# Cross attention of a fused decoder: where VectorE's maxima, an image's scaling and the weighted sums stand in the order of work

## The reference, cut to what matters

```python
q, k, v = x @ Wq + bq, y @ Wk + bk, y @ Wv + bv
weight = jax.nn.softmax(einsum('bhqd,bhkd->bhqk', q, k) / sqrt(32), axis=-1)
out = einsum('bhqk,bhkd->bhqd', weight, v)
x = _layernorm(x + out.transpose(0, 2, 1, 3).reshape(B, SQ, 256) @ Wo + bo)
```

## Time and profile before

| what | number |
| --- | --- |
| median of 3 runs | 2578.68 us (2573.37 to 2583.72) |
| the profiled execution's own time | 2584.56 us |
| its span in the profile | 2583.2 us |
| mean granted clock of TensorE | 0.906 of 2.4 GHz |
| busy: PE, DVE, ACT, POOL | 82%, 67%, 46%, 34% of the span |
| the block from its first maxima to its end | 1233.6 to about 1733 us |
| units 0 to 15 (first to last pair) | 1271.4 to 1712 us |

### The profile page before, as it was taken

How to read it: one execution, slowest core, us unless ns; L and a number is a source line. 1 busy time by engine, 2 the same in 40 slices (tenths; PEclk the granted TensorE clock), 3 DMA queues, 4 the chain that set the end, 5 groups by cost and what they waited for, 6 DMA issues and landing times. The chain is left out here.

```text
span 2583.2 us, 45827 instructions
## 1 busy us (share of the span) xinstructions
PE 2107.4 (82%) x17241; PEld 1348.7 (52%) x17241; DVE 1723.9 (67%) x3400; ACT 1191.5 (46%) x2208; POOL 872.3 (34%) x672
## 2 busy tenths in 40 slices
PE   5997579987589995887788989877787897787787
PEld 3554147874479993443344444444555554555544
DVE  4876977768966665666677777737677435777553
ACT  2132866646333332323245555445565434655552
POOL 2110024421056660012266767553221223221041
PEclk8998779999689997888899989988999998998999
DMA  4112024451351113222222322020000001000000
GB/s 145 44 49 53 1 82 132 135 171 55 128 220 50 51 46 125 76 82 89 76 75 72 94 70 70 22 76 34 1 1 1 25 1 51 1 1 1 33 9 25
DMA packets 107465, 159.63 MB, mean 62 GB/s; under 512 B 26064, under 2 KB 85236, under 8 KB 104180
## 3 DMA queue, kind: packets, MB, share of 16 engines
q1 hardware_dynamic: 102836, 144.64, 18.0%
q0 software_dynamic: 4416, 12.06, 1.6%
HBM read 109.42 MB, written 47.19 MB: 61 GB/s over the span
## 5 line engine op out<-in xcount | busy, mean ns | idle before, releaser
L2981 DVE TENSOR_REDUCE xa_max<-psum 128x1 f32<-128x1024 f32 (+1 forms) x256 | 246.4, 987 | 97.7 <-PE psum L2892 93.1
L3063 ACT ACTIVATE xa_work<-psum 128x1024 f32<-128x1024 f32 (+1 forms) x208 | 212.8, 1024 | 186.0 <-PE psum L2915 184.4
L3120 POOL TENSOR_TENSOR xa_ctx_f<-xa_ctx_f,xa_work 128x1024 f32<-128x1024 f32 x96 | 226.8, 2362 | 45.9 <-ACT xa_work L3063 37.9
L3297 PE MATMUL psum<-xa_c_parts,x_hl_f 128*128 128x512 bf16 x576 | 154.3, 417 | 63.3 <-ACT qk_raw_l L3505 24.8
L2892 PE MATMUL psum<-xa_key_rows,xa_query_rows 96*128 96x512 bf16 (+1 forms) x512 | 132.9, 352 | 36.9 <-DVE xa_max L2981 20.8
L1050 POOL TENSOR_TENSOR text_q<-text_q 128x512 bf16<-128x512 f32 x64 | 81.5, 1277 | 175.4 <-ACT text_q L1470 175.1
L2932 PE MATMUL psum<-xa_work,xa_values 128*32 128x128 f32 (+1 forms) x3328 | 140.7, 287 | 0.0
L2915 PE MATMUL psum<-xa_query_rows,xa_key_rows 98*128 98x512 bf16 (+1 forms) x416 | 130.3, 396 | 10.4 <-DVE xa_max L2981 10.4
L1802 PE MATMUL psum<-moe_rows,moe_w 128*128 128x256 bf16 x1104 | 130.4, 276 | 4.9 <-issue 4.9
L2061 ACT CAST x_ch<-moe_raw 128x512 bf16<-128x512 f32 x92 | 56.9, 618 | 158.7 <-DVE moe_raw L1976 158.2
L3297 PEld LDWEIGHTS psum<-xa_c_parts,x_hl_f 128*128 128x128 bf16 x576 | 56.3, 104 | 138.2 <-ACT qk_raw_l L3505 27.8
(11 more groups left out here) (482 smaller groups left out, 5118.7 us busy)
## 6 DMA issues: line engine op xcount, KB each, us to landing
text_q<-in_moe_w SPq DMA_DIRECT2D x64, 256.0 KB, 3.5
experts<-text_q SPq DMA_DIRECT2D x64, 256.0 KB, 2.8
moe_w<-experts SPq DMA_DIRECT2D x16, 1024.0 KB, 10.7
xa_key_rows<-cross_keys SPq DMA_DIRECT2D x48, 200.1 KB, 3.5
ctx_chunk<-in_ctxT SPq DMA_DIRECT2D x24, 300.0 KB, 3.0
cross_keys<-xa_k_hl SPq DMA_DIRECT2D x6, 800.5 KB, 3.7
moe_w<-pairs_out SPq DMA_DIRECT2D x8, 512.0 KB, 7.4
xa_ctx_f<-in_ctxT SPq DMA_DIRECT2D x4, 800.5 KB, 4.9
```

The source lines that it names most:

```text
L2981: v.tensor_reduce(t["maxes"][n % 2][:, qt * HU + a, part:part + 1], u.wide[:, 0:c1 - c0], AX.X, ALU.max).then_inc(*u.free)
L3063: act.activation(t["exps"][k % EXPS][0:rows], u.wide[0:rows].rearrange("p (m q) -> p m q", q=T), ACT.Exp, scale=1.0 / float(np.sqrt(np.flo ...
L3120: g.tensor_tensor(total, other, exps, ALU.add).then_inc(*s.added.up())
L3297: ins = pe.matmul(b.ap, x[:, i, h, w * P:(w + 1) * P], t["wqkv"][:, j, h, cols], start=(h, n) == (0, 0), stop=(h, n) == (1, 2))
```

## The change: what it does

It touches `cross_plan`, the norm's scaling and the order within a step.

```diff
+def reducing_work(step):
+    if step[0] == "maximum":
+        a, e = PARTS[step[4]]
+        return e - a + 160
+    return {"gather": 2500, "out": 700, "spread": 2000, "scale": 400, "cut": 1100, "subtract": 400}.get(step[0], 0)

 def cross_plan():
...
-    unit, lead = len(maxima) // UNITS_X, 3 * len(maxima) // UNITS_X // 2
+    lead = LATER + 2 * TPB * HU + 2
...
-            for lag, what in ((3, ("out", 0)), (4, ("out", 2)), (6, ("spread",)), (8, ("scale",)), (11, ("channels",))):
+            for lag, what in ((3, ("out", 0)), (4, ("out", 2)), (6, ("spread",)), (8, ("scale",)), (9, ("normal",)), (11, ("channels",))):
...
-    done = 0
+    total = sum(map(reducing_work, maxima)) + sum(reducing_work(step) for steps in late.values() for step in steps)
+    share, credit, done = total / (STEPS - KT), 0.0, 0
     for k in range(STEPS + BEHIND + 16):
-        if 0 <= k - BEHIND < STEPS:
-            plan.append(("product", k - BEHIND))
         plan += late.get(k, [])
+        credit += share - sum(map(reducing_work, late.get(k, [])))
         if k < STEPS:
             plan.append(("pair", k))
...
-        upto = min(len(maxima), unit * (k + 1) // KT)
-        plan += maxima[done:upto]
-        done = max(done, upto)
+        due = maxima.index(("subtract", (k + 2) // KT)) if ("subtract", (k + 2) // KT) in maxima else -1
+        while done < len(maxima) and (credit > 0 or done <= due):
+            plan.append(maxima[done])
+            credit -= reducing_work(maxima[done])
+            done += 1
+        if 0 <= k - BEHIND < STEPS:
+            plan.append(("product", k - BEHIND))
...
 cross_dve:
         elif kind == "scale":
...
             v.reciprocal(m.rstd[:, tiles], m.std[:, tiles]).then_inc(*s.v_step.up())
             v.wait_ge(*s.v_step.now())
-            for i in group(b):
-                ins = v.tensor_scalar(x[:, i, :], x[:, i, :], m.mv[:, i, 0:1], m.rstd[:, i:i + 1], ALU.subtract, ALU.mult)
-            ins.then_inc(*s.normed.up())
+            v.scalar_tensor_tensor(t["minus"][:, tiles], m.mv[:, tiles, 0], -1.0, m.rstd[:, tiles], ALU.mult, ALU.mult).then_inc(*s.centred.up())
 cross_act:
+        elif kind == "normal":
+            b, = step[1:]
+            act.wait_ge(*s.centred(b + 1))
+            for i in group(b):
+                x = m.x_tok[:, i, :]
+                ins = act.activation(x, x, ACT.Identity, scale=m.rstd[:, i:i + 1], bias=t["minus"][:, i:i + 1])
+            ins.then_inc(*s.normed.up())
```

More of the change, by code:

```diff
@@ L2751, in cross_attention @@
                  parts=ring("xa_parts", 2, [P, TPB, 2, HU], BF16), parts_t=ring("xa_parts_t", 2, [2 * HU, T], BF16),
-                 ident_b=sb("xa_ident_b", [P, P], BF16), rsum=ring("xa_rsum", 2, [P, ASKED]))
+                 ident_b=sb("xa_ident_b", [P, P], BF16), rsum=ring("xa_rsum", 2, [P, ASKED]),
+                 minus=sb("xa_minus_mean", [P, TILES]))
         work, spare = sb("xa_work", [P, EXPS * HU * T]), kept["ctx_f"][:].rearrange("p x s -> p (x s)")
@@ L2764, in cross_attention @@
         late = m.signals("late0_loaded late1_loaded late_high late_low late0_stored late1_stored", first=50)
-        s = m.signals("wo_loaded k_stored0 k_stored1 rows0 rows1 rows2 max0 max1 max2 v_step variance deviation normed "
+        s = m.signals("wo_loaded k_stored0 k_stored1 rows0 rows1 rows2 max0 max1 max2 v_step variance deviation centred normed "
                       "ones added biased cut x_high x_low in_high multiplied q_high q_stored")
@@ L3034, in cross_dve @@
             b, = step[1:]
-            x, tiles = m.x_tok, slice(b * TPB, (b + 1) * TPB)
+            tiles = slice(b * TPB, (b + 1) * TPB)
             v.wait_ge(*s.deviation(b + 1))
```

## The result

| | before | after |
| --- | --- | --- |
| median of 8 runs each on one chip | 2573.40 us (2571.51 to 2583.72) | 2590.59 us (2586.32 to 2596.96) |
| ratio of the medians, 95% interval | | 1.0063 [1.0046, 1.0081] |
| the profiled execution, its span | 2584.56, 2583.2 us | 2593.21, 2591.9 us |
| first pair of unit 0 | 1271.4 us | 1274.1 us |
| sum of units 4, 8 and 12 | 115.8 us | 99.2 us |

The change makes the kernel slower by 0.6%. The two profiled spans differ by 8.7 us, and the table accounts for them: +2.7 for the start, -16.6, -6.5, +27.8 (nine times 3.1, before rounding), +1.0, and +0.3 behind the block. The medians lie 17.2 us apart, since before's profiled execution was 11 us above the median of its 8 runs and after's 2.6 above. The first pair alone came anywhere from 1265.2 to 1272.5 us in the nine kernels with 27 entries ahead of it; the rest of those 11 us stays open.

The account below looks back on a forecast made before the run. TensorE was taken to bound the kernel, busy 23.34 of 24.7 us in an undisturbed unit. Terms -19.5 + 1.0 - 6 + 7 + 6 = -11.5 us against the median 2578.7 gave 2567.2 us, range 2540 to 2592.

Parts of the forecast that it names:

- Term 1: Units 4, 8 and 12, at image ends: shorter without VectorE's four scalings, -19.5 us in sum, bounds -6 and -28.
- The second stop: Image end in unit 4: TensorE's 3.0 us idle behind VectorE's scalings, predicted to go.
- The first stop: Image end in unit 4: TensorE's 2.90 us idle at ScalarE's table loads and root; stays, but -1.1 us, bounds 0 and -2.
- The stop at the gather: Unit 4's stop at the gather of the unit before, predicted to go, about -1.0 us.
- the second rival: Image ends: ScalarE becomes the wait, TensorE stops as long as for VectorE; sum +2, 2581 us; chance 20%.
- Term 2: Last image, its chain uncovered: scalings become one small instruction, a signal and 2.4 us on ScalarE, +1.0 us.
- Term 3: Units 0, 1 and the lead of 24 entries instead of 27: lead -2, unit 1 -3, unit 0 -1, sum -6 us.
- Terms 4 and 5: Undisturbed units, 12 and 14: idle time -15, cuts held by GpSimd's additions +22, net +7 us; clock after stops +6.
- the third rival: Cuts stop TensorE in every unit, GpSimd's additions holding both two-operand instructions; 28.5 us a unit, +17, 2596 us; chance 13%.
- The first rival: Cuts: GpSimd does not get in the way and the idle 1.36 us go everywhere; sum -39.5, 2539 us; chance 22%.
- Priced at nothing: Product at a step's end, `gather`'s wait, `subtract` two steps ahead in four units, `normal`'s wait: no cost expected.
- The cheap alternative: Cuts inside rows of additions pay next to nothing, by the 766 ns mean; sum some 28 us lower.

Follow-up runs that it names:

- the free cut: The cut's first and third instruction changed to read at most one SBUF operand, other values in PSUM; on after 2553.38 us (0.9909), on before 2565.11 us (0.9961).

## Why the prediction was wrong, point by point

The forecast was -11.5 us; the profiles show +8.7. The measured 2590.6 us still lies just inside the range of 2540 to 2592 us, which says little: the change went the other way, by a rival that had been given 13%. By its own terms:

**Term 1, right.** -19.5 predicted, -16.6 measured, and -18.8 with the free cut, which also takes the held cut out of these units (97.0 us in sum). The second stop went, as ScalarE's scaling alone removes it in all three units. Some of the gain is moved rather than made: these units hold 8 maxima fewer than before, which others carry now, and this the prediction did not count. The first stop hardly shortened: 2.90 us became 1.58 and 0.97, -0.35 where -1.1 was predicted, and 0.1 and 0.65 less in units 8 and 12. The clock came back from 0.87 to 0.95 in unit 4 and from 0.85 to 0.90 in unit 8, but fell from 0.95 to 0.90 in unit 12, whose cut is held. The stop at the gather, 1.05 us in each before, went in unit 4, as predicted; 0.59 and 0.66 us are left in units 8 and 12. ScalarE's share was over-priced: 595 ns each against the 589 of the earlier trace rows, but TensorE has no idle time behind it in unit 4, so +1.4 was nothing there. That, and a term of -16.6 where it had -6, refutes the second rival, ScalarE as the wait.

**Term 2, right.** +1.0 predicted, +0.9 measured (4.73 to 5.62 us).

**Term 3, units right, lead of the wrong sign.** Units 0 and 1 fell by 6.5 us (4 predicted), but by luck. The reason given was fewer maxima behind the cut, and these units hold 37 instead of 33. First and third instruction of their cuts took 3 us instead of 8, since the cut of unit 0 happened to pass freely; with free cuts the two units take 53.5 us in the old order and 55.4 with the change. The lead was priced at -2 and bounded at 0; the first pair came 2.7 us later. It was costed by three reductions only, and "`subtract` comes two steps ahead" was costed for four units, not for unit 0, where nothing lies between the transfer and the pair: 3.99 us of waiting. Not all of the 2.7 us is its price: from the block's first maximum to the first pair before took 39.0 us and after 39.8, and over all kernels it was 37.5 to 39.2 us with 27 entries and 38.4 to 41.7 with 24. Net -3.8 against -6.

**Terms 4 and 5, the step that failed.** +7 and +6 predicted for the cuts, the idle time and the clock; the nine units and unit 14 gave +28.8 (unit 12's cut is in term 1).

The mechanism of the hold was the one named: 12 of 16 third instructions were held, and the two that come just ahead of a gather, in units 4 and 8, escaped as written. Its reason, that the gap between the second and the third addition closes, was needed in the five cuts that began beside the second addition; the seven beside the first would have met the second addition in any case.

Five means of the nine undisturbed units give the sizes: 24.77 us (before), 24.28 (free cut), 23.95 (the product at the end as well, and ScalarE's scaling), 24.43 (the new placement as well), 27.87 (the held cut again, which is after). The forecast was +1.2 us a unit (13 us over eleven), and +3.1 came.

- The regained idle time, -1.36 us in each unit, is where most of the error lies. With free cuts the new placement is worth +0.48 us a unit (23.95 to 24.43). The stop of 0.96 us behind the gather did go, as the term said. What the term put at nothing is the work that the credit rule moves here: six of the nine units hold 17 maxima instead of 16, and with free cuts TensorE is busy for 23.8 to 24.1 us in these, for 23.2, 23.3 and 23.7 us in the three with 16, and for 23.1 to 23.2 us in all nine at the old rate, all at a clock of 1.00. The two stops of 1.2 us for the free cut's own banks are another part of the +0.48.
- The held cut, 2.0 us and 1.5 us of clock in four of eleven units, so 2.5 us in the mean. Measured are 3.4 us a unit with its clock (27.87 - 24.43), of which before already paid 0.5 (24.77 - 24.28). Of the two ends, unit 3 and unit 1, the nearer row was unit 1: 3.87 us of TensorE's idle time at a clock of 0.89. The reason given for taking less, a step with one maximum behind the cut, did not save it; in unit 10 TensorE still idled for 3.51 us.

So the third rival came true in its mechanism: additions without gaps, both instructions held, a mean of 27.9 us a unit, above its threshold of 26.9, and clock 0.94 in most. It said every unit at 28.5 us, which is more than came: units 6 and 11 took 25.5 us at a clock of 1.00, and its sum was +17 us where the profiles show +8.7. Its objection, that a stop opens GpSimd's gap again, was not borne out: besides units 4 and 8 only the cut ahead of the first pair and the one in unit 0 passed freely. The first rival, no blocking, falls with it.

**Priced at nothing, and not nothing.** The product at the end of a step gave -9 us by itself (0.9965), and 0.3 us a unit beside free cuts, in the good direction. The prediction looked only for what a later product might delay. What it moves forward, pairs and late work by one product, it left out: with free cuts the stop behind the gather is 0.96 us with the product first and 0.65 or 0.72 with it last. Most of the -9 us is not this, but the shift of two cuts against the additions in units 0 and 1.

**The wrong mean was weighed.** The cheap alternative rested on the mean of 766 ns, which belongs to the cut's first instruction. The third (315 ns before) was the one to ask about: a hold of the first alone costs 0.5 us a unit, the two together 3.4.

## What to carry to other kernels

Before work is moved to another place in the order, look for instructions in it that another engine's instructions can hold, and at each of them in the rows one by one: a mean of 315 ns was one at 2.24 us and thirteen near 0.17 us, by luck of place. Remove the sensitivity first (here operands in PSUM for three 8-column instructions), then judge the placement; that order would have shown that the placement was worth nothing: with the free cut it gives 0.9909, the old rate 0.9886 and 0.9904. Count the work that a new placement moves into the other units before its gain is booked. And an experiment that frees one stop is to be compared with the kernel that differs from it in nothing else.

## What the runs showed of the hardware that was not expected

- An instruction of 8 columns costs a whole GpSimd instruction, 2.25 us, if its operands lie in SBUF and an addition of 2.36 us has just begun, and 166 ns with the same values in PSUM and SBUF, beside the same additions. This held for the middle instruction of the cut too, which reads one tensor: 2.26 us once, and 1.20 to 1.22 us seven times beside halves of 1.27 us. The reduction that reads one SBUF tensor and writes PSUM was not held (176 ns); why the two differ was not tried.
- VectorE's subtract-and-multiply of 128x256, which has one SBUF tensor and two scalars of one column, takes 0.40 or 0.41 us beside no addition and up to 2.57 us when one runs. Its means of 1131 and 670 ns tell only how many of the 16 were held. Which of its operands matters was not tried.
- In after the granted clock goes with the size of TensorE's stop behind the cut: 1.00 in units 6 and 11 (1.46 us), 0.94 or 0.89 in the seven with 1.86 to 3.51 us, and 1.00 in unit 3, which had 0.94, once its cut was free.
